# Experts of a two-layer macaron network: routing weights spread by DMA instead of TensorE, gelu left in PSUM, other places for the routing work

## The chip, the cores and the metric

The kernel runs on one core of a Trainium2 chip. The metric is the device time of one execution in microseconds (us); lower is better. PE is TensorE, ACT is ScalarE, DVE is VectorE, POOL is GpSimd, and SP is SyncE, which issues the DMAs.

## The reference

The input `x` has 4096 tokens of 128 channels. Six residual stages follow each other: a gated feed-forward, a time-mixing attention, the feed-forward again, a mixture of experts, a flow attention, and the mixture of experts again. The change is in the fourth and the sixth, which share weights:

```
xn = (x - mu) * rsqrt(var + EPS) * ln_gamma + ln_beta
abel_out = gelu(xn @ abel_w + abel_b)
logits = xn @ moe_gate_w + moe_gate_b
topw, topi = top_k(logits, 2);  topw = softmax(topw)
w_dense = sum(one_hot(topi, 8) * topw[..., None], axis=-2)
h  = gelu(einsum('bsd,edh->ebsh', xn, ew1) + eb1)     # 8 experts, 256 hidden
eo = einsum('ebsh,ehd->ebsd', h, ew2) + eb2
moe_out = einsum('ebsd,bse->bsd', eo, w_dense)        # then three 128x128 rotations
gate = sigmoid(concat(abel_out, moe_out) @ gc_w + gc_b)
x = x + 0.5 * (residual + abel_out * (1 - gate) + moe_out * gate)
```

## The kernel before

Every stage goes through the tokens in 8 chunks of 512 (`NCH`), channels on the partitions. Each engine has its own program, and semaphores tie them together; the order on an engine is written out by hand. The residual `X` stays in SBUF, and SP stores it chunk by chunk in the last stage.

In an expert stage (`experts`, once on each engine) a chunk has 16 units `u` (`NU`): 8 experts of two halves of 128 hidden channels. A unit goes through five steps:

- PE: the first product, three float16 matmuls of 512 columns (`three`, lines L1457 to L1459), into one of banks 0 to 2 (`MM1_BANK`);
- ACT: gelu out of that bank into the buffer `mo.hf` (L980), called gelu(u) below;
- DVE: times the routing weight, `mo.hw` (L1296), called hw(u);
- ACT: the float16 copy `mo.hhi` (`high`, L975), called high(u), in ACT's program behind gelu(u+1);
- POOL: the remainder `mo.hlo` (`low`, L772); then PE's second product (`second`, again three matmuls) into bank 5, `SKEW` units behind the first.

The routing weight of a token must stand on all 128 partitions. PE makes it: for each expert a matmul with the selection matrix `sel` (L1639) copies one row of `mo.wT` over bank 3 or 4. `mo.wT` holds 16 rows in float16 (high and low parts of 8 weights).

`pipeline` runs each step of the loop over three chunks: `lead` (chunk i+1: normalise into `Z`, turn it on PE, take `mo.xn`, `mo.xhi`, `mo.xlo` from bank 6, update `X` by L1315, make the logits and the top-2 chain on DVE, L1328 to L1343, then the weights, L1347 to L1351, and their turned copy `mo.wT`, L1362), `mid` (the 16 units of chunk i), and `lag` (chunk i-1: `mo.dm` L1290, `mo.gs` L1302, the gate on PE and ACT, `mo.r` L1320 and L1323, the addition to `X` L1187, in the fourth stage with the norm's statistics behind it, L1150). At which unit each of these stands is a number in the program (`u == 8`). Of the 8 chunks, six pass through a full step; the first has no lag, the last no lead. At the last unit PE waits until `X` is updated (bank 6 must be free), then makes the Abel product, whose gelu (L998) and scaled copy (L1001) ACT does before high(15).

## Time and profile before

| | us |
|---|---|
| median of 3 runs | 1070.07 (1068.48 to 1070.43) |
| profiled execution, its own time | 1070.72 |
| its span | 1069.0 |
| busy in the span: PE, DVE, ACT, POOL | 878.7, 727.8, 657.3, 604.1 |
| fourth stage, hw(0) of the first chunk to the last pair of hw | 335.0 to 565.6 |
| sixth stage, hw(0) of the first chunk to hw(15) of the last | 829.9 to 1055.7 |

The execution's own time is 1.7 us above its span. No engine is busy all the time: an expert stage is a chain that goes round between engines, and what matters is which engine's program is without a gap at which place of a chunk.

### The profile page before, as it was taken

The numbers are of one execution on the slowest core, as the hardware profiler recorded it, in microseconds if no ns is written. First come the engines' busy times: TensorE is split into PE (matmuls) and PEld (weight loads), VectorE is DVE, ScalarE is ACT, GpSimd is POOL, SyncE is SP. The second block draws the span as 40 slices with busy tenths as digits, with TensorE's granted clock in tenths as the row PEclk, the third lists the DMA queues.
The fourth block names the chain that finished last, engine by engine and source line by source line (L and its number), as shares of the span: only waits on it lengthen the run. The fifth ranks groups of instructions, "written<-read, shape, count | busy, mean of one in ns | idle before, by whom it ended". The sixth has DMA issues, their size and how long they took to land.

```text
span 1069.0 us, 14730 instructions
## 1 busy us (share of the span) xinstructions
PE 878.7 (82%) x3958; PEld 463.0 (43%) x3958; DVE 727.8 (68%) x1580; ACT 657.3 (61%) x1171; POOL 604.1 (57%) x579
## 2 busy tenths in 40 slices
PE   7789677689936988899895698999973899999997
PEld 6644333274412344444442355555532344444443
DVE  6945389945634677887764267777783777777784
ACT  2177499857725777777773443333322778787874
POOL 4244775665484656666676154444446566666664
PEclk9989888769977999999997899999996899999998
DMA  8000000000000000000000000000000000000000
GB/s 201 10 2 0 0 0 1 0 1 2 0 0 1 1 1 1 0 0 0 0 1 1 0 1 0 1 1 1 2 1 0 1 1 11 10 10 10 10 10 20
DMA packets 17932, 8.26 MB, mean 8 GB/s; under 512 B 4168, under 2 KB 17884, under 8 KB 17884
## 3 DMA queue, kind: packets, MB, share of 16 engines
q1 hardware_dynamic: 17884, 7.70, 2.8%
q8 instruction: 21, 0.34, 0.1%
q14 instruction: 27, 0.22, 0.1%
HBM read 5.60 MB, written 2.10 MB: 7 GB/s over the span
## 4 chain that ended last, share of the span: by engine, by line
POOL 33%; issue 29%; PE 18%; DVE 12%; ACT 5%; POOLq 1%; SPq 1%; DVEq 0%; DMA 0%; ACTq 0%
POOL arena L772 19%; POOL arena L792 5%; POOL arena L735 4%; PE bank L1457 3%; PE bank L1458 3%; PE bank L1459 3%; PE bank L1692 3%; POOL rstd L692 2%; POOL v L700 1%; DVE stats L1150 1%; DVE X L1315 1%; ACT arena L975 1%; ACT Z L891 1%; DVE arena L1242 1%; DVE arena L1296 1%
## 5 line engine op out<-in xcount | busy, mean ns | idle before, releaser
L772 POOL TENSOR_TENSOR arena<-arena 128x512 f16<-128x512 f32 x256 | 300.4, 1184 | 181.8 <-ACT arena L975 181.1
L1296 DVE TENSOR_TENSOR arena<-arena,bank 128x512 f32<-128x512 f32 x256 | 172.3, 683 | 93.3 <-ACT arena L980 89.7
L975 ACT ACTIVATE arena<-arena 128x512 f16<-128x512 f32 x256 | 160.4, 627 | 65.4 <-DVE arena L1296 45.2
L980 ACT ACTIVATE arena<-bank,eb 128x512 f32<-128x512 f32 x256 | 173.8, 680 | 34.9 <-PE bank L1459 32.7
L799 POOL TENSOR_TENSOR arena<-arena 128x512 f32<-128x512 f32 (+1 forms) x24 | 32.7, 1374 | 117.7 <-DVE arena L1421 90.0
L1458 PE MATMUL bank<-arena,ew1hi 128*128 128x512 f16 x256 | 99.0, 387 | 0.0
L1457 PE MATMUL bank<-arena,ew1hi 128*128 128x512 f16 x256 | 99.0, 387 | 0.0
L1459 PE MATMUL bank<-arena,ew1lo 128*128 128x512 f16 x256 | 98.9, 386 | 0.0
L1457 PE MATMUL bank<-arena,ew2hi 128*128 128x512 f16 x256 | 97.6, 381 | 0.8 <-POOL arena L772 0.8
L1458 PE MATMUL bank<-arena,ew2hi 128*128 128x512 f16 x256 | 97.5, 381 | 0.0
L1459 PE MATMUL bank<-arena,ew2lo 128*128 128x512 f16 x256 | 97.5, 381 | 0.0
L735 POOL TENSOR_TENSOR arena<-arena 128x512 f16<-128x512 f32 x48 | 54.9, 1159 | 64.4 <-ACT arena L905 64.4
L1639 PE MATMUL bank<-arena,sel 128*128 128x512 f16 x128 | 49.8, 389 | 33.1 <-DVE arena L1296 23.6
L1699 PE MATMUL bank<-arena,until 128*128 128x512 f32 x128 | 63.0, 615 | 14.2 <-DVE arena L1377 13.1
L1457 PE MATMUL bank<-arena,f0hi 128*128 128x512 f16 x144 | 56.9, 395 | 17.0 <-POOL arena L735 13.6
L792 POOL TENSOR_TENSOR arena<-arena 128x1024 f32<-128x1024 f32 x32 | 61.7, 1950 | 0.0
L1211 DVE SCALAR_TENSOR_TENSOR arena<-bank,arena 128x512 f32<-128x512 f32 x48 | 33.0, 691 | 36.0 <-ACT arena L912 34.7
L1388 DVE SCALAR_TENSOR_TENSOR arena<-arena,bank 128x1024 f32<-128x1024 f32 x16 | 19.5, 1221 | 55.3 <-PE bank L1692 55.3
L891 ACT ACTIVATE Z<-X,nbias,rstd 128x128 f32<-128x128 f32 (+1 forms) x128 | 52.5, 487 | 7.4 <-POOL pool_spare L705 7.4
L1541 PE MATMUL bank<-ident,Z 128*128 128x128 f32 x192 | 31.5, 290 | 30.6 <-ACT Z L891 18.1
L1458 PE MATMUL bank<-arena,f0hi 128*128 128x512 f16 x144 | 56.6, 393 | 0.0
L1459 PE MATMUL bank<-arena,f0lo 128*128 128x512 f16 x144 | 56.5, 392 | 0.0
(286 smaller groups left out, 1922.2 us busy)
## 6 DMA issues: line engine op xcount, KB each, us to landing
X<-in_L_attn_x_dram SPq DMA_DIRECT2D x8, 256.0 KB, 4.4
out_dram<-X SPq DMA_DIRECT2D x8, 256.0 KB, 2.3
arena<-in_L_ffn_ew_dram SPq DMA_DIRECT2D x2, 512.0 KB, 6.7
arena<-in_L_ffn_ew_dram SPq DMA_DIRECT2D x1, 1024.0 KB
arena<-in_L_ffn_gens_dram SPq DMA_DIRECT2D x1, 192.0 KB, 2.3
arena<-in_L_ffn_w_gate_dram SPq DMA_DIRECT2D x1, 192.0 KB, 2.7
arena<-in_L_ffn_w_up_dram SPq DMA_DIRECT2D x1, 192.0 KB, 2.8
arena<-in_L_ffn_w_down_dram SPq DMA_DIRECT2D x1, 192.0 KB, 3.9
```

The source lines that it names most:

```text
L735: pool.tensor_tensor(f0.hlo[:, u, :], f0.h[:, u % 2, :], f0.hhi[:, u, :], ALU.subtract).then_inc(S.hlo, 1)
L772: pool.tensor_tensor(mo.hlo[:, u % 8, :], mo.hw[:, u % 4, :], mo.hhi[:, u % 8, :], ALU.subtract).then_inc(S.hlo, 1)
L792: pool.tensor_tensor(fl.kv[:, b, :].rearrange("p (h m d) -> p h m d", d=HD, m=HD), key.to_broadcast([P, HEADS, HD, HD]), value.to_broadcas ...
L891: last = A(Z[:, zp, t * P:(t + 1) * P], X[:, bass.ds(tile * P, P)], ACT.Identity, bias=bias[:, bass.ds(tile, 1)], scale=scale[:, bass.ds(t ...
L975: A(mo.hhi[:, u % 8, :], mo.hw[:, u % 4, :], ACT.Copy).then_inc(S.hhi, 1)
L980: A(mo.hf[:, u % 4, :], bank[MM1_BANK[u]][:, :], ACT.Gelu, scale=1.0 / WS, bias=eb1[:, u:u + 1]).then_inc(S.gelu, 1)
L1296: TT(mo.hw[:, u % 4, :], mo.hf[:, u % 4, :], bank[3 + (u // EB) % 2][:, :], ALU.mult)\
L1457: mm(dst, whi, xhi, start=start, stop=False, skip_group_check=True)
L1458: mm(dst, whi, xlo, start=False, stop=False, skip_group_check=True)
L1459: return mm(dst, wlo, xhi, start=False, stop=stop, skip_group_check=True)
L1639: mm(bank[3 + e % 2][:, :], sel[:, e, :], mo.wT[:, p, :], start=True, stop=True)\
L1699: mm(bank[5 + h], until[:, :], fl.kv[:, b, h * CH:(h + 1) * CH], start=True, stop=True)\
```

## The change

- The weight rows are now float32, 8 of them. DVE makes twice the weight (two small operations fewer, L1349 and L1351 go); the factor 0.5 moves into `mo.dm`. PE turns it, and DVE copies 8 rows of 512 into `mo.wT`.
- SP (`routes`) writes these rows to a scratch tensor in DRAM, waits for it, and issues four DMAs that each read two experts' rows onto all 128 partitions of the new buffer `mo.wB` (512 KB each). DVE waits for the first at unit 0, the next at units 4, 8 and 12. The eight `sel` matmuls a chunk go, and so do `sel` and `ident16` in the setup.
- Banks 3 and 4 are free, so the first products use five banks. ACT writes gelu back into the bank, and DVE multiplies out of it; a bank is free after hw instead of after gelu. `SKEW` is 6.
- The bias of the second product is one float32 matmul (`ebw`) instead of two float16 ones.
- In `lead`, other units: normalise in units 0 and 1 (two tiles each); PE's turn 5 to 3; `xn`, `xhi`, `xlo` 6 to 4; logits and top-2 chain 8 to 5; tanh 10 to 7; weights 11 to 8; PE's turn of the weights 14 to 10; `mo.wT` 14 to 11; the update of `X` 7 to 12.
- SP's loop over the stores is unrolled, with `routes` of the next chunk ahead of each wait and store.

```diff
-SKEW = 5
-MM1_BANK = (0, 1, 2, 0, 1, 2, 0, 1, 2, 0, 1, 2, 0, 1, 2, 1)
+SKEW = 6
+MM1_BANK = (0, 1, 2, 3, 4, 0, 1, 2, 3, 4, 0, 1, 2, 3, 4, 2)
...
-            with sp.Fori(0, NCH) as c:
+            def routes(c):
+
+                sp.wait_ge(MO.wT, c + 1)
+                for k in range(E // 2):
+                    after(sp, MO.wB[k], 16 * c)
+                sp.dma_start(wrows[c % 2], mo.wT[0:E, c % 2, :]).then_inc(MO.wd, 16)
+                sp.wait_ge(MO.wd, 16 * (c + 1))
+                after(sp, MO.hw, NU * (c - 1))
+                for k in range(E // 2):
+                    sp.dma_start(mo.wB[:, c % 2, 2 * k:2 * k + 2, :],
+                                 wrows[c % 2, 2 * k:2 * k + 2, :].partition_broadcast(P)).then_inc(MO.wB[k], 16)
+
+            for c in range(NCH):
+                routes(c)
+            routes(NCH)
+            for c in range(NCH):
+                if c + 1 < NCH:
+                    routes(NCH + c + 1)
                 sp.wait_ge(MO.x, c + (NCH + 1))
-                sp.dma_start(out_parts[:, :, bass.ds(c, 1), :], X4[:, :, bass.ds(c, 1), :]).then_inc(stored, 16)
+                sp.dma_start(out_parts[:, :, c:c + 1, :], X4[:, :, c:c + 1, :]).then_inc(stored, 16)
...
-                            after(act, S.hw, NU * i + u - 3)
-                            A(mo.hf[:, u % 4, :], bank[MM1_BANK[u]][:, :], ACT.Gelu, scale=1.0 / WS,
+                            A(bank[MM1_BANK[u]][:, :], bank[MM1_BANK[u]][:, :], ACT.Gelu, scale=1.0 / WS,
                               bias=eb1[:, u:u + 1]).then_inc(S.gelu, 1)
                             if u:
                                 high(i, u - 1)
-                        if lead and mid and u < TILES:
-                            normalise(i + 1, 1 - p, S.z, first, number, [u])
-                        if lead and u == 6:
+                        if lead and mid and u < TILES // 2:
+                            normalise(i + 1, 1 - p, S.z, first, number, [2 * u, 2 * u + 1])
+                        if lead and u == 4:
                             act.wait_ge(S.tr, i + 2)
                             A(mo.xn, bank[6][:, :], ACT.Copy).then_inc(S.xn, 1)
                             A(mo.xhi[:, 1 - p, :], bank[6][:, :], ACT.Copy).then_inc(S.xhi, 1)
...
+                            if u % (2 * EB) == 0:
+                                dve.wait_ge(S.wB[u // (2 * EB)], 16 * i + 16)
                             after(dve, S.hlo, NU * i + u - 3)
-                            TT(mo.hw[:, u % 4, :], mo.hf[:, u % 4, :], bank[3 + (u // EB) % 2][:, :], ALU.mult)\
+                            TT(mo.hw[:, u % 4, :], bank[MM1_BANK[u]][:, :], mo.wB[:, p, u // EB, :], ALU.mult)\
                                 .then_inc(S.hw, 1)
 
                         if lag and u == 4:
...
                             dve.wait_ge(S.g0, i)
                             STT(out=mo.gs, in0=mo.dm, scalar=gcw[:, 1:2], in1=mo.g0[:, n, :], op0=ALU.mult,
                                 op1=ALU.add).then_inc(S.gs, 1)
-                        if lead and u == 6:
+                        if lead and u == 4:
...
-                        if lead and u == 7:
+                        if lead and u == 12:
...
-                        if lead and u == 8:
+                        if lead and u == 5:
                             own.at(i + 1)
...
-                        if lead and u == 11:
+                        if lead and u == 8:
                             dve.wait_ge(S.th, i + 2)
                             share = mo.th.rearrange("p (t o) -> p t o", o=1).to_broadcast([P, TILES, E])
                             own.link(TT(mo.wd, mo.diff, share, ALU.mult))
-                            own.link(TT(mo.wd, mo.wd, mo.sum, ALU.add))
-                            own.link(TS(mo.wp[:, :, 0:E], mo.wd, 0.5, None, ALU.mult))
                             own.close()
-                            STT(out=mo.wp[:, :, E:2 * E], in0=mo.wd, scalar=0.5, in1=mo.wp[:, :, 0:E], op0=ALU.mult,
-                                op1=ALU.subtract).then_inc(S.wpair, 1)
+                            TT(mo.wd, mo.wd, mo.sum, ALU.add).then_inc(S.wpair, 1)
...
-                        if lead and u == 14:
+                        if lead and u == 11:
                             dve.wait_ge(S.wpT, i + 2)
-                            dve.tensor_copy(mo.wT[0:2 * E, n, :], bank[7][0:2 * E, 0:CH // 2].bitcast(F16))\
-                               .then_inc(S.wT, 1)
+                            after(dve, S.wd, 16 * i)
+                            dve.tensor_copy(mo.wT[0:E, n, :], bank[7][0:E, :]).then_inc(S.wT, 1)
...
-                TAIL = {0: (11,), 1: (12,), 2: (13, 14), 3: (15,)}
+                TAIL = {0: (10,), 1: (11, 12), 2: (13, 14), 3: (15,)}
 
                 def step(i, p, lead, mid, lag):
                     n = 1 - p
                         pe.wait_ge(S.hlo, NU * c + u + 1)
                         if u == 0:
                             after(pe, S.dm, c)
-                            mm(bank[5][:, :], ebhi[:, :], mo.wT[:, cp, :], start=True, stop=False,
-                               skip_group_check=True)
-                            mm(bank[5][:, :], eblo[:, :], mo.wT[:, cp, :], start=False, stop=False,
+                            mm(bank[5][:, :], ebw[:, :], mo.wT[:, cp, :], start=True, stop=False,
                                skip_group_check=True)
                         three(bank[5][:, :], ew2hi[:, u, :], ew2lo[:, u, :], mo.hhi[:, u % 8, :],
                               mo.hlo[:, u % 8, :], start=False, stop=(u == NU - 1)).then_inc(S.mm2, 1)
                         if mid:
                             if u == 0:
                                 pe.wait_ge(S.xlo, i + 1)
-                            if u % EB == 0:
-                                e = u // EB
-                                if e == 0:
-                                    pe.wait_ge(S.wT, i + 1)
-                                after(pe, S.hw, NU * i + EB * (e - 1))
-                                mm(bank[3 + e % 2][:, :], sel[:, e, :], mo.wT[:, p, :], start=True, stop=True)\
-                                    .then_inc(S.wb, 1)
-                            after(pe, S.gelu, NU * i + bank_free(u))
+                            after(pe, S.hw, NU * i + bank_free(u))
                             three(bank[MM1_BANK[u]][:, :], ew1hi[:, u, :], ew1lo[:, u, :], mo.xhi[:, p, :],
                                   mo.xlo[:, p, :]).then_inc(S.mm1, 1)
                         for v in TAIL.get(u, ()) if lag else ():
                             second(i - 1, n, v)
                         if mid and u >= SKEW:
                             second(i, p, u - SKEW)
-                        if lead and u == 5:
+                        if lead and u == 3:
...
-                        if lead and u == 8:
+                        if lead and u == 5:
                             pe.wait_ge(S.xn, i + 2)
```

On DVE, in the full step of the loop, this is what stood between `mo.xlo` (L1306) and the start of the top-2 chain (L1328) before; L1296 is hw:

```order
L1306 TENSOR_TENSOR arena<-bank,arena 128x512
L1293 REGISTER_ALU
L1296 TENSOR_TENSOR arena<-arena,bank 128x512
L1315 ISA x2
L1315 TENSOR_SCALAR X<-X,keep,shift 128x128
...
L1315 TENSOR_SCALAR X<-X,keep,shift 128x128
L1293 REGISTER_ALU
L1294 REGISTER_ALU
L1296 TENSOR_TENSOR arena<-arena,bank 128x512
L1328 TENSOR_TENSOR arena<-bank,gate_b4 128x32
```

Now, from `mo.gs` (L1298) over `mo.xlo` (L1302) to the chain (L1324 to L1339); hw is L1292:

```order
L1298 SCALAR_TENSOR_TENSOR arena<-arena,gcw 128x512
L1301 REGISTER_ALU
L1302 TENSOR_TENSOR arena<-bank,arena 128x512
L1288 REGISTER_ALU
L1292 TENSOR_TENSOR arena<-bank,arena 128x512
L1324 TENSOR_TENSOR arena<-bank,gate_b4 128x32
...
L1339 TENSOR_TENSOR arena<-arena 128x32
L71 REGISTER_ALU
L1288 REGISTER_ALU
L1292 TENSOR_TENSOR arena<-bank,arena 128x512
```

The chain stands behind hw(5), directly after `mo.gs` and `mo.xlo`, and the update of `X` has left this place. It is now here, between hw(12) and hw(13), behind the copy of the weight rows (L1356) and ahead of the addition to `X` (L1182):

```order
L1356 COPY arena<-bank 8x512
L1288 REGISTER_ALU
L1292 TENSOR_TENSOR arena<-bank,arena 128x512
L1311 ISA
L1311 REGISTER_ALU
L1311 TENSOR_SCALAR X<-X,keep,shift 128x128
...
L1288 REGISTER_ALU
L1292 TENSOR_TENSOR arena<-bank,arena 128x512
L1182 ISA
L1182 SCALAR_TENSOR_TENSOR X<-bank,X 128x512
```

So the last four units of a chunk have the two longest pieces of DVE's other work between them.

On SP, the end of the program before is a loop of 8 stores:

```order
L598 UNCONDITIONAL_BRANCH
L598 ISA
L600 ISA
L600 DMA out_dram<-X 128x4x128
L598 REGISTER_ALU
L598 COMPARE_AND_BRANCH
```

Now, in the sixth stage (`wrows` is the scratch tensor, and the four DMAs of L601 go into `mo.wB`):

```order
L611 DMA out_dram<-X 128x4x128
L597 DMA wrows<-arena 8x512
L601 DMA arena<-wrows 128x1024 x4
L611 DMA out_dram<-X 128x4x128
L597 DMA wrows<-arena 8x512
L601 DMA arena<-wrows 128x1024 x4
```

A write of weight rows has moved behind a store, and the store waits for the addition to `X` of the chunk before. In the fourth stage nothing is stored, and only L597 and L601 follow each other.

## Rows read from the trace of the kernel before

**Rows 1.** The chain of waits: start us, us, what.

```profile
440.63 2.55 issue
...
470.77 2.55 issue
...
933.73 2.55 issue
...
962.96 2.55 issue
```

**Rows 2.** Stretches, fourth stage and end of the sixth; busy (instructions), PE clock.

```profile
core 0: us, PE busy (x) PEld busy (x) DVE busy (x) ACT busy (x) POOL busy (x), PEclk, DMA share, GB/s
454.30:484.50 30.20, 27.10 (x133) 12.77 (x131) 23.72 (x57) 23.16 (x43) 18.94 (x17) 1.00 0.00 0
1034.00:1055.70 21.70, 21.70 (x102) 10.12 (x101) 14.06 (x21) 17.89 (x31) 16.74 (x15) 1.00 0.02 6
```

**Rows 3.** Timeline of DVE, one chunk: start us, us, line, op, [idle before].

```profile
454.34 0.69 DVE L1296 TENSOR_TENSOR arena<-arena,bank 128x512 f32<-128x512 f32 x1 [2.40 <-ACT arena L980]
...
460.48 1.51 DVE L1302 SCALAR_TENSOR_TENSOR arena<-arena,gcw 128x512 f32<-128x512 f32 x1
...
465.46 2.81 DVE L1315 TENSOR_SCALAR X<-X,keep,shift  x4
...
468.79 0.18 DVE L1328 TENSOR_TENSOR arena<-bank,gate_b 128x32 f32<-128x32 f32 x1
...
471.93 1.28 DVE L1296 TENSOR_TENSOR arena<-arena,bank 128x512 f32<-128x512 f32 x2 [0.22 <-DVE arena L1343]
473.13 0.69 DVE L1320 SCALAR_TENSOR_TENSOR bank<-bank,arena 128x512 f32<-128x512 f32 x1
...
475.06 0.69 DVE L1347 TENSOR_TENSOR arena<-arena 128x32 f32<-128x32 f32 x1
475.79 0.19 DVE L1348 TENSOR_TENSOR arena<-arena 128x32 f32<-128x32 f32 x1
...
478.58 0.68 DVE L1187 SCALAR_TENSOR_TENSOR X<-bank,X 128x512 f32 x1
...
480.48 0.69 DVE L1296 TENSOR_TENSOR arena<-arena,bank 128x512 f32<-128x512 f32 x1
```

**Rows 4.** Timeline of ACT, the start of that chunk.

```profile
451.06 0.63 ACT L975 ACTIVATE arena<-arena 128x512 f16<-128x512 f32 x1 [0.81 <-DVE arena L1296]
...
452.93 0.61 ACT L975 ACTIVATE arena<-arena 128x512 f16<-128x512 f32 x1
453.45 0.67 ACT L980 ACTIVATE arena<-bank,eb 128x512 f32<-128x512 f32 x1
454.02 0.48 ACT L891 ACTIVATE Z<-X,nbias,rr 128x128 f32 x1
454.41 0.67 ACT L980 ACTIVATE arena<-bank,eb 128x512 f32<-128x512 f32 x1
```

**Rows 5.** Timeline of PE, that chunk.

```profile
451.60 0.39 PE L1639 MATMUL bank<-arena,sel 128*128 128x512 f16 x1 [1.31 <-DVE arena L1362]
451.82 0.38 PE L1457 MATMUL bank<-arena,ew1hi 128*128 128x512 f16 x1
...
465.21 1.02 PE L1656 MATMUL bank<-arena,ones 128*128 128x512 f32 x2
```

**Rows 6.** DMA issues, KB each, median us from issue to landing.

```profile
out_dram<-X SPq DMA_DIRECT2D x8, 256.0 KB, 2.3
arena<-in_L_ffn_ew_dram SPq DMA_DIRECT2D x2, 512.0 KB, 6.7
...
tvec<-n_L_attn_time_mix_r_dram SPq DMA_DIRECT2D x1, 0.5 KB, 2.1
```

**Rows 7.** Timeline of SP, issue of one DMA.

```profile
7.25 0.43 SPq L567 DMA_DIRECT2D tvec<-n_L_attn_time_mix_r_dram  x1
```

**Rows 8.** Timeline of DVE, before the fourth stage, POOL idle.

```profile
326.11 1.11 DVE L1315 TENSOR_SCALAR X<-X,keep,shift 128x128 f32<-128x128 f32 x4
```

More of the change, by code:

```diff
@@ L181, in macaron_kernel @@
         ablo = sb("ablo", [P, P], F16)
-        ebhi = sb("ebhi", [P, P], F16)
-        eblo = sb("eblo", [P, P], F16)
-        sel = sb("sel", [P, E, P], F16)
+        ebw = sb("ebw", [P, P])
         gamma = sb("gamma", [P, 1])
@@ L260, in macaron_kernel @@
         sm.eb2 = a.take([P], parts=E)
-        sm.eb2T = a.take([2, E])
+        sm.eb2T = a.take([E])
         sm.G = a.take([NROT, P])
@@ L278, in macaron_kernel @@
         mo.xlo = a.take([2, CH], F16)
-        mo.hf = a.take([4, CH])
+        mo.wB = a.take([2, E, CH])
         mo.hw = a.take([4, CH])
@@ L297, in macaron_kernel @@
         mo.wd = a.take([TILES, E])
-        mo.wp = a.take([TILES, 2 * E], F16)
-        mo.wT = a.take([2, CH], F16)
+        mo.wT = a.take([2, CH])
         a = Arena(arena)
@@ L358, in macaron_kernel @@
         S0.rots = sem("setup_rots")
-        S0.turned = sem("setup_turned")
         S0.gtp = sem("setup_gtp")
@@ L437, in macaron_kernel @@
         MO.gelu = sem("moe_gelu")
-        MO.wb = sem("moe_wb")
+        MO.wd = sem("moe_wd")
+        MO.wB = [sem(f"moe_wB{k}") for k in range(E // 2)]
         MO.hw = sem("moe_hw")
@@ L633, in setup @@
                           allow_small_or_imprecise_dtypes=True).then_inc(S0.consts, 1)
-                pool.wait_ge(S0.pool, 7)
-                pool.affine_select(out=sel[:, :, :], in_=sel[:, :, :], compare_op=ALU.not_equal, fill=1.0, base=0,
-                                   pattern=[[-1, E], [0, P]], channel_multiplier=1).then_inc(S0.pool, 1)
+                pool.wait_ge(S0.pool, 5)
                 pool.affine_select(out=blockones[:, :], in_=blockones[:, :], compare_op=ALU.is_ge, fill=0.0,
@@ L657, in bias_parts @@
                 chain = Chain(pool, S0.bias)
-                chain.base = 9
+                chain.base = 6
                 pool.wait_ge(S0.w_flow, 16 * N_FLOW)
@@ L846, in setup @@
                 for r in range(NROT):
-                    act.wait_ge(S0.rtp, r + 1)
-                    A(sm.rr[:, r, P:2 * P], bank[5 + r][:, P:2 * P], ACT.Copy).then_inc(S0.turned, 1)
+                    act.wait_ge(S0.gtp, r + 2)
+                    A(sm.rr[:, r, P:2 * P], bank[5 + r][:, P:2 * P], ACT.Copy).then_inc(S0.gt, 1)
                 act.wait_ge(FF.tr, 1)
@@ L858, in fold_a @@
                 act.wait_ge(S0.small, 1)
-                for n in range(2):
-                    A(sm.eb2T[:, n, :], bank[FOLD.m][:, 0:E], ACT.Copy).then_inc(S0.eb2T, 1)
+                A(sm.eb2T, bank[FOLD.m][:, 0:E], ACT.Copy).then_inc(S0.eb2T, 1)
                 for g in range(NU // TILES):
@@ L867, in fold_a @@
                     if g == 1:
-                        act.wait_ge(S0.rp, 1)
-                        A(sm.R, bank[FOLD.m][:, 0:P], ACT.Copy).then_inc(S0.r, 1)
+                        act.wait_ge(S0.mtp, 2)
+                        A(sm.R, bank[FOLD.m][:, 0:P], ACT.Copy).then_inc(S0.mt, 1)
             def fold_b():
@@ L879, in fold_b @@
                 act.wait_ge(S0.consts, N_CONST)
-                A(ebhi[0:2 * E, :], bank[FOLD.small][0:2 * E, P:2 * P], ACT.Copy, scale=WS)
-                A(sm.MT[0:2 * E, :], bank[FOLD.small][0:2 * E, P:2 * P], ACT.Copy, scale=WS).then_inc(S0.fhi, 1)
+                A(ebw[0:E, :], bank[FOLD.small][0:E, P:2 * P], ACT.Copy, scale=WS).then_inc(S0.fhi, 1)
             def normalise(c, zp, sem, first, number, tiles=range(TILES)):
@@ L992, in step @@
                             A(bank[6][:, :], bank[6][:, :], ACT.Tanh, scale=0.5, bias=gcbh[:, :]).then_inc(S.tg, 1)
-                        if lead and u == 10:
+                        if lead and u == 7:
                             act.wait_ge(S.dtop, i + 2)
@@ L1278, in experts @@
             def experts(S, first, number):
-                own = Chain(dve, S.own, 11)
+                own = Chain(dve, S.own, 9)
                 dve.wait_ge(S.zero, 1 if first == 0 else 2)
@@ L1513, in fold_a @@
                         pe.wait_ge(S0.mt, 1)
-                        mm(bank[FOLD.m][:, 0:P], sm.MT, rot(2), start=True, stop=True).then_inc(S0.rp, 1)
+                        mm(bank[FOLD.m][:, 0:P], sm.MT, rot(2), start=True, stop=True).then_inc(S0.mtp, 1)
                 pe.wait_ge(S0.folds, 2)
@@ L1533, in fold_b @@
                     last.then_inc(S0.fm, 1)
-                mm(bank[FOLD.small][0:2 * E, P:2 * P], sm.eb2T.rearrange("p a b -> p (a b)"), sm.R, start=True,
-                   stop=True).then_inc(S0.fm, 1)
+                mm(bank[FOLD.small][0:E, P:2 * P], sm.eb2T, sm.R, start=True, stop=True).then_inc(S0.fm, 1)
             def turn_chunk(z, zp, sem_z, value, sem_out, to=0):
@@ L1668, in step @@
                             last.then_inc(S.rT, 1)
-                        if lead and u == 14:
+                        if lead and u == 10:
                             pe.wait_ge(S.wpair, i + 2)
-                            turned = bank[7][0:2 * E, 0:CH // 2].bitcast(F16)
                             for t in range(TILES):
-                                last = tr(turned[:, t * P:(t + 1) * P], mo.wp[:, t, :], ident16[:, :])
+                                last = tr(bank[7][0:E, t * P:(t + 1) * P], mo.wd[:, t, :], ident[:, :])
                             last.then_inc(S.wpT, 1)
```

51 lines of the change are left out of this document (18 added, 33 removed).

## Prediction

> **What bounds the kernel now.** I read the chain of waits first. In the expert stages it names POOL and "issue" again and again, at one distance: 470.77 - 440.63 = 30.14 us in the fourth stage, 962.96 - 933.73 = 29.23 us in the sixth [rows 1]. That is a full chunk, and POOL stands there only as the last link. In the view of stretches PE is busy 27.1 of 30.2 us at the full clock, DVE 23.7, ACT 23.2, POOL 18.9 [rows 2], so nobody is the bound alone, and I went to the timelines to see where each engine has no gap. DVE has none from about 464 to 482: update of `X`, top-2 chain, `mo.r`, weights, addition to `X` with statistics, copy of `mo.wT` [rows 3]. Then PE, which has waited 1.31 for that copy, starts the next chunk with `sel` [rows 5], DVE idles 2.40 before hw(0) [rows 3], and PE, nearly without a gap, leads to the turned chunk, `mo.xlo` and DVE again. The round is DVE 17, PE and ACT 13. Only in the last chunk of a stage, which has no lead, is PE busy throughout, 21.70 of 21.70 [rows 2].
>
> **PE's part.** 8 `sel` matmuls and 2 bias ones go, each one step of 451.82 - 451.60 = 0.22 [rows 5]: 2.2 a chunk. One float32 matmul of 512 columns comes, two passes, 1.02 [rows 5], 0.9 of it its own, and 0.1 for the wider turn. Net -1.2 a chunk. It shortens a full chunk only if PE is in the round, and the wait for `mo.wT`, which put it there, is gone. So I go round the new program with the old durations.
>
> **The new round, fourth stage.** ACT first. From high(14) at 451.06 over the Abel gelu, its copy and high(15) at 452.93 to gelu(0) at 453.45 are 2.39 [rows 4], unchanged. Then up to gelu(4): four gelus of 0.57, three copies of 0.52, and the four tiles of the normalise, 0.39 each (454.41 - 454.02) [rows 4], now all in units 0 and 1: 5.4. PE needs 33 matmuls of 0.22 and one turn for gelu(4), some 7.9 from the chunk's start on PE; high(14) comes 1.3 after that start (PE's wait for `X` at the last unit is over before DVE's statistics, 1.9, are), so ACT is at gelu(4) after 1.3 + 2.4 + 5.4 = 9.1 and sets it. gelu to hw takes 0.89 (454.34 - 453.45) [rows 3, 4], and hw(14) to high(14) 0.7 (480.48 against 451.06 + 30.14). ACT's stretch is 9.4.
>
> From hw(4) to hw(14) DVE has hardly a gap: 10 hw of 0.60 (473.13 - 471.93 for two), 6.0; `mo.gs` 1.6 (1.51 in its row); `mo.xlo` 0.6; the top-2 chain 471.93 - 468.79 = 3.1, I take 3.2; the weights, two operations, 0.73 and 0.2 [rows 3], with some blocking 1.1; `mo.r` 475.06 - 473.13 less one hw, 1.3; the copy of 8 float32 rows 0.6, like other 512-column reads from PSUM; `X` 468.79 - 465.46 less one hw, 2.7; addition and statistics 480.48 - 478.58 = 1.9 [rows 3]. Two new gaps come in. During the chain ACT stands in high(6), and gelu(8) is behind it, so after hw(6) and hw(7) DVE waits 1.1 for gelu(8); before hw(10), ACT's tanh of the gate costs 0.6. In the old order `mo.r` and the weights filled such holes. Sum 20.7, and a chunk 9.4 + 20.7 = 30.1: no gain against 30.14, though DVE is rid of 1.4 and PE of 1.2. I give this walk 0.5 a chunk both ways.
>
> The spread is hidden there. `mo.wT` is ready near hw(12); write and first broadcast take some 6, and 9.5 are left before hw(0) is wanted. Four broadcasts of 512 KB fit in 30 us even at the loaded rate of 6.7 each [rows 6].
>
> **Sixth stage.** No statistics: 1.3 less. But there SP goes store by store: weights of the next chunk are ready before the addition to `X`, yet their write stands behind a store that waits for this addition. From the end of the addition: waking SP 0.1, issue of the store 0.43 [rows 7], write of the rows 2.1 (the row of 0.5 KB) and 0.3 for the 256 KB of the store ahead of it [rows 6], waking SP and DVE 0.2, and the broadcast L: 3.1 + L. L is bounded by 2.3 (256 KB on an idle queue) and 6.7 (512 KB on a full one) [rows 6]; the queue is idle here, so I take 3.2, a fifth of the way from the idle row to the loaded one (512 KB are twice the idle row's bytes). The round is then hw(0) to hw(4) 5.2 (0.8 to high(0), 3.5 of ACT, 0.9), hw(4) to hw(13) 20.7 - 0.6 - 1.9 = 18.2, hw(13) and addition 1.3, spread 6.3: 31.0 against 29.23, +1.8. With L 2.3 it is 30.1, +0.9; with 6.7 34.5, +5.3. What is queued behind hw(0) on DVE is everything; ACT stops in high(0) after gelu(1), and PE after five first products.
>
> The Trainium skill has a price for this ("DMA: Bandwidth & Descriptors", section "Anatomy of one DMA"): about 2.0 us fixed and the bytes over 436 GB/s, for GpSimd's queue, most of it the confirmation of the write, longest for HBM. An estimate by that page is 2.0 for the write and 3.2 for the broadcast, which gives this sum, 1073; by the 6.7 of [rows 6] it would be 1094. The row of 0.5 KB, 2.1, agrees with the page's fixed part.
>
> **Ends and setup.** First chunk: the chain comes before the update of `X`, which alone takes 1.1 [rows 8], and two small operations fewer; PE waits no longer for weights, but hw(0) waits for the spread: -0.7 each, from -2.5 to +2.5. Last chunk: PE's, so its 1.3 of matmuls (1.2 without the turn) and the 1.3 wait [rows 5] go, -2.6; in the sixth stage PE also gives back 0.9 of the late hw(0), -3.5. In the setup POOL's `sel` goes where POOL waits anyway; fewer copies in the weight folding, -0.3.
>
> **Sum.** Fourth stage -0.7 + 0 - 2.6 = -3.3; sixth -0.7 + 6 x 1.8 - 3.5 = +6.6; setup -0.3: +3.0 on the execution's 1070.7, which stands 0.65 above the median: 1073.
>
> **A rule that speaks for more.** Beside POOL the four tiles of `X` take 2.81 [rows 3], alone 1.11 [rows 8], so 1.7 of DVE's 20.7 is blocking, about 0.9 for each of two POOL operations, and it hangs on where these fall. The skill ("SBUF — State Buffer", section "Who interferes with whom") says that such operations and POOL's exclude each other for a whole instruction. By it each of the chain's cast, `mo.gs`, the two weight operations and `X` could be hit in the new places; three more hits are 2.6 a chunk and 30 in all, one is 0.9 and 11. No row shows where POOL's operations will fall, so this is in the range, not in the sum.
>
> **Rivals.**
> - *The stretches overlap (faster).* If the five banks let PE and ACT run so far ahead that DVE's gaps fill and hw(4) isn't held by ACT, a chunk falls to what PE allows: 27.1 - 1.2 and about 1.3 of waiting for the update of `X` at the last unit, with 0.8 of other stalls 28.0. Then 6 x 2.1 + 6 x 1.2 + 8 at the ends is -28: 1042; half of it, 1056. For it: PE's busy share and 2.6 less work on two engines. Against it: ACT does gelu and high strictly in turn. It decides from the point where ACT's and DVE's stretches together are under 28.
> - *The spread is hidden in the sixth stage too.* With L near 2.3 and the walk 0.3 too long, gains at the ends and losses cancel: 1070.
> - *The broadcast is slow.* All 128 partitions read the same 4 KB; if that takes the loaded 6.7, it is +21 more: 1094. One more blocking by POOL a chunk, +11, ends at 1084.
> - *The change doesn't do what it says:* PE cannot run ahead because its second products still wait for POOL; that is the walk's result already.
>
> **How the numbers follow.** My forecast, 1073 (its own range 1067 to 1081), 0.50; overlap 0.22; hidden 0.16; slow broadcast or more blocking 0.12. The range goes from 1056 to 1088. 0.2% (2.1 us) is about what a measurement tells from no change. Faster: 0.22, some of "hidden" and a little of the forecast, 0.28. Same: 0.17. Slower: 0.55.
>
> **What would show it.** Right: chunks of 30 us in the fourth and 31 in the sixth stage; DVE waiting for a DMA before hw(0) in the sixth only, by 1 to 3 us; DVE gaps before hw(8) and hw(10); PE idle before the logits and before the Abel product; the last chunk about 3 shorter. Wrong: a chunk under 29 in the fourth (the walk), or no wait for the DMA in the sixth (L or the order on SP), or waits at units 4, 8 and 12 (bandwidth).

## The result, and the profile after

The changed kernel takes 1080.26 us, median of 4 runs (1079.92 to 1083.16), against 1069.28 (1068.21 to 1070.43) for the kernel before on the same chip: ratio 1.0092, 95% interval 1.0058 to 1.0126. It is slower, inside the range, and 7 us above the forecast of 1073.

The spans of the two profiled executions, 1069.0 and 1078.7, were compared stretch by stretch, by the starts of the first hw (`hw(0)`) of each chunk; a last chunk is counted to the end of its hw(15):

| stretch | before | after | difference | forecast |
|---|---|---|---|---|
| up to 300 us, no expert work | | | +2.8 | -0.3 |
| fourth stage, to hw(0) of its second chunk | | | +0.2 | -0.7 |
| its six middle chunks | 6 x 30.10 | 6 x 30.37 | +1.6 | 0 |
| its last chunk | 22.44 | 19.87 | -2.6 | -2.6 |
| fifth stage, and sixth to hw(0) of its second chunk | | | +2.5 | -0.7 |
| six middle chunks of the sixth | 6 x 29.19 | 6 x 30.52 | +8.0 | +10.8 |
| its last chunk | 22.36 | 19.60 | -2.8 | -3.5 |

They add to 9.7, the difference of the spans.

The view of stretches of the changed kernel, for a middle chunk of the fourth and of the sixth stage (us of the stretch, busy time of each engine, granted clock), answers to [rows 2]:

```profile
457.44:487.74 30.30, 27.42 (x124) 12.78 (x123) 23.24 (x54) 23.20 (x44) 18.62 (x16) 0.94 0.19 69
951.75:982.33 30.58, 25.86 (x125) 12.39 (x123) 21.92 (x49) 23.17 (x44) 18.53 (x16) 1.00 0.24 78
```

PE, the first figure, has only 25.86 us to do in the sixth stage, 1.2 less than in [rows 2] as forecast. In the fourth it shows 27.42 for the same work, and the granted clock, 0.94, is not full. That was not forecast. DVE's timeline of the same chunk of the fourth stage, in the places of [rows 3]:

```profile
458.29 0.69 DVE L1292 TENSOR_TENSOR arena<-bank,arena 128x512 f32<-128x512 f32 x1 [2.67 <-ACT bank L975]
...
463.49 0.69 DVE L1292 TENSOR_TENSOR arena<-bank,arena 128x512 f32<-128x512 f32 x1 [0.21 <-ACT bank L975]
464.10 1.74 DVE L1298 SCALAR_TENSOR_TENSOR arena<-arena,gcw 128x512 f32<-128x512 f32 x1
...
470.14 1.42 DVE L1292 TENSOR_TENSOR arena<-bank,arena 128x512 f32<-128x512 f32 x2 [0.19 <-DVE arena L1339]
472.25 0.69 DVE L1292 TENSOR_TENSOR arena<-bank,arena 128x512 f32<-128x512 f32 x1 [0.69 <-ACT bank L975]
...
474.07 0.19 DVE L1345 TENSOR_TENSOR arena<-arena 128x32 f32<-128x32 f32 x1
...
475.98 0.69 DVE L1292 TENSOR_TENSOR arena<-bank,arena 128x512 f32<-128x512 f32 x1 [0.98 <-ACT bank L975]
...
479.71 2.56 DVE L1311 TENSOR_SCALAR X<-X,keep,shift  x4
```

The two gaps that the walk named are there, before hw(8) and hw(10). But behind the second stands PE. Its timeline shows a wait for the input of the logits, and then every matmul at twice its time: the bias product takes 1.91 and the next steps 0.43 in place of 0.22 [rows 5]. The row below them is the view of stretches of that time, and its granted clock is a half (1.2 GHz):

```profile
464.56 1.06 PE L1643 MATMUL bank<-gate_g,arena 128*128 128x8 f32 x8 [1.82 <-ACT arena L983]
...
466.18 1.91 PE L1615 MATMUL bank<-arena,ebw 128*128 128x512 f32 x2
467.89 0.63 PE L1450 MATMUL bank<-arena,ew2hi 128*128 128x512 f16 x1
468.32 0.63 PE L1451 MATMUL bank<-arena,ew2hi 128*128 128x512 f16 x1
```

```profile
466.10:469.40 3.30, 3.30 (x7) 1.10 (x6) 3.12 (x20) 1.29 (x2) 2.31 (x2) 0.50 0.00 0
```

All six middle chunks of the fourth stage and its first have such a stretch, and none of the sixth's middle ones. But the same wait is in those too, for 1.82 us as well, and what follows it there runs at the full clock:

```profile
961.58 1.06 PE L1643 MATMUL bank<-gate_g,arena 128*128 128x8 f32 x8 [1.82 <-ACT arena L983]
962.50 0.38 PE L1450 MATMUL bank<-arena,ew1hi 128*128 128x512 f16 x1
...
963.14 1.02 PE L1615 MATMUL bank<-arena,ebw 128*128 128x512 f32 x2
```

So the wait alone does not decide it. What else does, no run here isolates.

In the sixth stage the chain of waits shows the spread, link by link, from the addition to `X` to hw(0):

```profile
978.63 0.69 DVE X L1182
979.32 0.02 issue
979.34 0.39 SPq L611
...
979.89 1.89 DMA wrows<-arena
981.79 0.02 issue
981.80 4.29 DMA arena<-wrows
...
986.21 0.70 DVE arena L1292
```

And the view of waits puts 37.1 us on it, in seven waits, six in the sixth stage and one in the fourth stage's first chunk:

```profile
DVE arena L1292 <- DMA arena<-wrows: 37.1, 7, 5.6
```

### The profile page after: what moved, and what is told of

The parts are those of the page before. It is cut to its first block, busy times and chain, and to the rows that moved or that the text cites. A ratio compares the mean times of both kernels' runs of the same rounds, so it can differ in the third digit from the quotient of the medians.

```text
span 1078.7 us, 14118 instructions
## 1 busy us (share of the span) xinstructions
PE 871.6 (81%) x3821; PEld 462.6 (43%) x3830; DVE 720.1 (67%) x1548; ACT 656.9 (61%) x1169; POOL 596.3 (55%) x572
## 4 chain that ended last, share of the span: by engine, by line
issue 28%; POOL 24%; DVE 18%; PE 17%; ACT 8%; DMA 3%; SPq 1%; DVEq 1%; POOLq 0%; ACTq 0%
POOL arena L770 10%; POOL arena L790 4%; POOL arena L733 4%; DVE arena L1292 3%; PE bank L1674 3%; PE bank L1450 2%; DMA arena<-wrows 2%; PE bank L1452 2%; PE bank L1451 2%; ACT bank L975 2%; POOL rstd L694 2%; ACT arena L971 2%; ACT Z L887 1%; POOL v L702 1%; DVE stats L1145 1%
## 5 line engine op out<-in xcount | busy, mean ns | idle before, releaser
L1292 DVE TENSOR_TENSOR arena<-bank,arena 128x512 f32<-128x512 f32 x256 | 171.9, 684 | 121.6 <-ACT bank L975 76.8
L975 ACT ACTIVATE bank<-bank,eb 128x512 f32<-128x512 f32 x256 | 167.0, 653 | 41.0 <-PE bank L1452 36.1
L1370 DVE TENSOR_TENSOR arena<-bank,arena 128x512 f32<-128x512 f32 x64 | 42.4, 686 | 12.9 <-PE bank L1681 12.9
```

Source lines behind the costliest of these rows:

```text
L975: A(bank[MM1_BANK[u]][:, :], bank[MM1_BANK[u]][:, :], ACT.Gelu, scale=1.0 / WS, bias=eb1[:, u:u + 1]).then_inc(S.gelu, 1)
L1292: TT(mo.hw[:, u % 4, :], bank[MM1_BANK[u]][:, :], mo.wB[:, p, u // EB, :], ALU.mult)\
L1370: TT(fl.prod[:, b % 2, h * CH:(h + 1) * CH].rearrange("p (h m d) -> p h m d", d=HD, m=HD), bank[5 + h].rearrange("p (h m d) -> p h m d", d ...
```

## The experiments

Ratios are to the kernel before, which ran beside each; "chunk" is a middle one, from the profile. `after` stands for the changed kernel.

**SP's order (`sp_ahead`).** In the sixth stage:

```diff
+            routes(NCH + 1)
             for c in range(NCH):
-                if c + 1 < NCH:
-                    routes(NCH + c + 1)
+                if c + 2 < NCH:
+                    routes(NCH + c + 2)
```

> In the sixth stage SP issues the weights' write and broadcasts of the next chunk but one ahead of the store that waits for the addition to X, everything else as changed. Theory (SP's order costs the sixth stage): DVE's wait of 5.5 us for the DMA before hw(0) goes; ACT's own start of a chunk then ends the wait after about 2.7 us as in the fourth stage, and DVE's stretch is that of the fourth less 1.3 of statistics: chunk 29.1 against 30.6 us, 6 x 1.5 = 9 us, and 1 at the last chunk: about 1071. Rival (the DMA's wait only hides what ACT or PE would make DVE wait anyway, and the unit order of DVE sets 30.6): chunk stays within 0.3, 1079 to 1080.

Measured: 1067.24, ratio 0.9979 (0.9964 to 0.9994). No DVE wait for the DMA is left in the middle chunks; hw(0) waits 2.53 for ACT. The theory's wait is gone, and the time is 4 us below what it said: the chunks are 29.06, 27.89, 28.12, 29.35, 28.00 and 29.17, two kinds, where one of 29.1 was expected. The view of stretches for one of each:

```profile
888.32:916.21 27.89, 25.41 (x124) 12.37 (x122) 21.95 (x49) 23.17 (x43) 18.55 (x16) 1.00 0.24 76
944.33:973.68 29.35, 27.54 (x126) 12.87 (x124) 22.26 (x49) 23.32 (x43) 18.64 (x16) 0.94 0.29 89
```

The long ones are those with part of the time at the half clock. In this run's fourth stage five middle chunks of six have it and take 30.1 to 30.7; the one without takes 29.2. So the half clock seemed to cost some 1.2 us a chunk, and the next runs asked whether that is cause or sign.

**Three banks (`banks3`).** `MM1_BANK` as before the change.

> The changed kernel with the first products in three banks (as before) in place of five, skew and everything else as changed. Theory (PE running ahead is worth nothing, since ACT stands in high(0) and DVE has the long stretch): chunks 30.4 and 30.6 as with five, 1080 within 2 us. Rival (the five banks do carry part of the round, since PE's run ahead hides its wait for the turned chunk and the logits): 0.5 to 1 us more for each of the 12 middle chunks, 1086 to 1092.

Measured: 1088.57 (1079.48 to 1091.18), ratio 1.0158 (1.0104 to 1.0213). The rival, in one stage: the fourth is about as with five banks (29.1 to 30.4), the sixth has 30.7 to 33.5, and its granted clock is where the time is:

```profile
919.50:953.20 33.70, 30.10 (x127) 13.80 (x126) 22.49 (x49) 23.92 (x45) 18.59 (x16) 0.90 0.22 71
```

This looks like the rival. But the changed kernel, run again (below), had three such chunks with five banks too, and its interval overlaps this one. That five banks hold the clock through the wait before hw(0) more often than three is left open; that they are worth more than a few us here is not shown.

**DVE's stretch (`fill`).** The update of `X` goes from unit 12 to unit 1, and in the fourth stage:

```diff
-                            if first == 0:
-                                finish_x(i - 1, first, bank[6][:, :], 0.5, S.x, i)
-                            else:
-                                add_to_x(i - 1, first, bank[6][:, :], 0.5, S.x, number)
+                            add_to_x(i - 1, first, bank[6][:, :], 0.5, S.x, 0 if first == 0 else number)
+                        if lag and u == NU - 1 and first == 0:
+                            wait_apart(dve, S.x, i)
+                            tile_stats(i - 1 - first)
```

> The changed kernel with two pieces of DVE's long stretch moved to where DVE idles: the update of X from unit 12 to unit 1, and in the fourth stage the statistics from unit 13 behind hw(15), where DVE waits 2.7 us for the next chunk. Theory (the round is DVE's stretch from hw(4) to hw(14) and ACT's from there): X leaves 2.6 in the fourth and 1.7 in the sixth stage, of which about 1 comes back as later hw(2) and hw(3), the statistics leave 1.1: the fourth stage's chunk falls from 30.4 to about 28.2, the sixth's from 30.6 to about 29.9, together 17 us: 1063. Rival (PE, with the logits' wait of 1.8 and the turn behind the later ACT, becomes the bound): fourth stage 29.5, sixth 30.6, 1075.

Measured: 1066.03, ratio 0.9966 (0.9945 to 0.9986); fourth stage 28.0 to 28.6, about as the theory had it. `X` is also cheaper in unit 1, away from POOL's operations: 1.11 in place of 2.56. The sixth stage, where the theory had 29.9, stays at 30.1 to 30.7, with one of 32.8: DVE finished earlier, but hw(0) still waits for the DMA, and now the half clock has come in there too (0.94 in a middle chunk).

**Logits later on PE (`logits_late`).** The block of the logits goes from the end of unit 5 to unit 6, behind its first product.

> The changed kernel with PE's logits one unit later, behind the first product of unit 6, so that PE waits less for ACT's copy (1.8 us in front of the logits, after which the granted clock fell to a half for some microseconds in every middle chunk of the fourth stage). Theory (the walk's 30.1 against the 30.4 measured is this lower clock): granted clock full, chunk 30.1, sixth stage unchanged, about 1078. Rival (PE is outside the round, the clock costs nothing, the 0.3 is elsewhere): chunk 30.4, 1080; or, if the chain on DVE starts later for it, 0.3 a chunk more, 1084.

Measured: 1071.57, ratio 1.0012 (0.9999 to 1.0026). Fourth stage 28.9 to 29.5 in the three middle chunks at the full clock, 29.7 to 29.9 in the three that still have a stretch at the half. The mechanism held and its size did not. The profiled execution is 12.2 us shorter than that of the changed kernel: 5.3 are the middle chunks of the fourth stage, where the theory had 2 by taking 0.3 for what the clock costs, and 4.8 lie ahead of the stage, where the two kernels are the same.

**More work for PE (`warm`).** Cause or sign, in one edit:

```diff
+                        if lead and mid and u == 5:
+                            for w in range(6):
+                                mm(bank[7][:, :], ew1hi[:, w, :], mo.xhi[:, p, :], start=True, stop=True)
                         if lead and u == 5:
                             pe.wait_ge(S.xn, i + 2)
```

> The changed kernel with six extra matmuls of 512 columns (1.3 us at the full clock, written to a bank that the logits overwrite) on PE in front of its wait for the logits' input, where it idles 1.8 us. Order, places, DMA and SP as changed. Theory (this idle time takes PE's clock to a half for 3.4 us in each middle chunk of the fourth stage, and the half clock itself costs the chunk 1.2 us: the run with SP's order had one chunk without it, of 29.2 against 30.4): the clock stays full, the fourth stage's chunk falls to 29.2 though PE has more to do, the sixth's stays at 30.6, about 1072. Rival (the late logits cost, not the clock): chunk 30.4 or, by the extra 1.3 on PE, up to 30.9: 1080 to 1084.

Measured: 1068.85 (1066.78 to 1072.89), ratio 0.9998 (0.9984 to 1.0012). PE does six matmuls more in each such chunk, which nobody needs, and the kernel takes 10 us less than without (by the ratios, 0.9998 and 1.0092). 6.8 of them are the fourth stage's middle chunks. The rest isn't shown to be the edit's: the profiled executions also differ by 2.5 ahead of the stage and by 4.3 between hw(15) of the fourth stage and the first copy of `mo.wT` in the sixth, where the code is the same, and that second stretch takes anything from 256.3 to 261.3 us in the thirteen profiles with the changed setup. The middle chunks of the fourth stage are 28.9 to 29.3 (the first 29.6), the sixth's 30.2 to 30.9. PE's rows in the place of those above, and the stretch of one chunk:

```profile
456.95 1.46 PE L1642 MATMUL bank<-arena,ew1hi 128*128 128x512 f16 x6
458.94 1.06 PE L1646 MATMUL bank<-gate_g,arena 128*128 128x8 f32 x8 [0.53 <-ACT arena L983]
...
460.50 1.02 PE L1615 MATMUL bank<-arena,ebw 128*128 128x512 f32 x2
```

```profile
451.81:481.09 29.28, 27.42 (x131) 12.90 (x130) 22.82 (x54) 23.03 (x44) 18.42 (x16) 1.00 0.24 83
```

The logits start 1.06 us after hw(4) here and 1.07 in the changed kernel (464.56 - 463.49). So the input comes no later than before, and the late input costs nothing; what follows at the half clock does. In both stages of this run no middle chunk has a stretch at the half clock. The theory holds.

**First broadcast halved (`first_small`).** Experts 0 and 1 in broadcasts of their own.

> The changed kernel with the weights of experts 0 and 1 in broadcasts of their own (256 KB each), the others in pairs as before. Theory (hw(0) in the sixth stage and in each stage's first chunk waits for issue, write and the first broadcast in a row, and of its 4.3 us about half goes with the bytes): the wait before hw(0) falls from 5.5 to about 4.0, the sixth stage's chunk from 30.6 to about 29.3 if nothing else is late, 8 chunks x 1.3 = 10 less, 1070. Rival (the 4.3 us are mostly fixed, or the four queued broadcasts share the DMA engines from the start): at most 0.5 a chunk, 1076 to 1080; or expert 1 is late at hw(2) and gives it back.

Measured: 1076.10, ratio 1.0055 (1.0034 to 1.0076). The wait before hw(0) falls from 5.5 to 4.6 in the sixth stage, so a broadcast of 256 KB needs about 0.9 us less than one of 512 KB, and by that difference more than half of 4.3 us is not bytes (an estimate; no run issues one broadcast alone, so what the ones queued behind it take is in it). In the middle chunks nothing of it arrives: they are 30.1 to 31.2, and five of six now have a stretch at the half clock:

```profile
948.28:979.15 30.87, 27.54 (x125) 13.00 (x123) 22.41 (x49) 23.20 (x43) 18.59 (x16) 0.94 0.23 77
```

**Old places (`places_before`).** The routing and the update of `X` in the units of before, all else changed.

> The changed kernel (DMA for the weights, gelu in PSUM, five banks) with the routing and the update of X in the units where they stood before: turn 5, logits and chain 8, weights 11, turn and copy of the weights 14. Theory (the spread takes about 6.5 us from the copy to hw(0), and from unit 14 there are only 3.4, so the DMA's wait comes into every chunk of both stages; what was moved is what hides it in the fourth): both stages wait for the DMA before hw(0), chunk about 31.5 to 32.5 in the fourth and about 31 in the sixth, about 1090. Rival (the old places suit the round, the new gaps before hw(8) and hw(10) cost as much as the spread): 30.4 in the fourth, 1078 to 1082.

Measured: 1094.85, ratio 1.0232 (1.0215 to 1.0249). Chunks 31.8 to 32.5 and 30.5 to 32.2; the wait for the DMA is now in 15 places, both stages:

```profile
DVE arena L1292 <- DMA arena<-wrows: 73.2, 15, 5.9
```

The theory holds. The new places hide the spread in the fourth stage, as the prediction said, and save some 11 to 15 us, by the two measurements of the changed kernel.

**Gelu in SBUF (`gelu_sbuf`).** Four buffers as before; PE's bank comes free after the gelu.

```diff
-                            A(bank[MM1_BANK[u]][:, :], bank[MM1_BANK[u]][:, :], ACT.Gelu, scale=1.0 / WS,
+                            after(act, S.hw, NU * i + u - 3)
+                            A(mo.hf[:, u % 4, :], bank[MM1_BANK[u]][:, :], ACT.Gelu, scale=1.0 / WS,
...
-                            TT(mo.hw[:, u % 4, :], bank[MM1_BANK[u]][:, :], mo.wB[:, p, u // EB, :], ALU.mult)\
+                            TT(mo.hw[:, u % 4, :], mo.hf[:, u % 4, :], mo.wB[:, p, u // EB, :], ALU.mult)\
...
-                            after(pe, S.hw, NU * i + bank_free(u))
+                            after(pe, S.gelu, NU * i + bank_free(u))
```

> The changed kernel with the gelu's output in SBUF again (four buffers), so that PE's next use of a bank waits for the gelu and no longer for hw; DMA, five banks and places as changed. Theory (PE's waits for banks are outside the round; a gelu to SBUF takes 0.68 in place of 0.65, some 0.1 for the four in ACT's stretch, 0.5 for the chunk): chunks 30.4 to 30.6 and 30.6 to 30.8, 1080 to 1082. Rival (banks that come free one operation earlier keep PE fed while hw(0) is late, or fill its waits and save the clock in the fourth stage): 29.3 in the fourth stage, 1072.

Measured: 1126.00, ratio 1.0520 (1.0505 to 1.0535). Both expectations missed by over 40 us. hw now reads two operands from SBUF (`arena<-arena`), where it had one in PSUM (`arena<-bank,arena`). The groups of hw and of POOL's `low` in this kernel, then in the changed one:

```profile
L1294 DVE TENSOR_TENSOR arena<-arena 128x512 f32<-128x512 f32 x256 | 228.7, 912 | 113.7 <-ACT arena L977 77.3 <-DMA arena<-wrows 30.2 <-issue 4.3
L771 POOL TENSOR_TENSOR arena<-arena 128x512 f16<-128x512 f32 x256 | 334.1, 1319 | 205.3 <-ACT arena L972 203.2
```

```profile
L1292 DVE TENSOR_TENSOR arena<-bank,arena 128x512 f32<-128x512 f32 x256 | 171.9, 684 | 121.6 <-ACT bank L975 76.8
L770 POOL TENSOR_TENSOR arena<-arena 128x512 f16<-128x512 f32 x256 | 297.2, 1170 | 190.4 <-ACT arena L971 186.8
```

hw takes 0.91 us on the mean (0.67 to 1.68) in place of 0.68, `low` 1.32 in place of 1.17. The Trainium skill ("SBUF — State Buffer", section "Who interferes with whom") has this rule: a VectorE operation with two inputs in SBUF contends with a GpSimd operation that reads SBUF, one with at most one, outside the modes that take both of VectorE's ports, does not. The trace agrees: with one input in PSUM none of the 256 hw takes over 0.70. Of the 46 us between the profiled executions 33 are in the middle chunks and 13 in the two last ones. The half clock is in most of them too (all but one of the middle chunks and both last ones), and no run separates the two; the one middle chunk without it takes 33.5, against 31.0 in the same place of the changed kernel. Once the weights lie in SBUF, the gelu in PSUM is what keeps the change from costing 5%. That a gelu to PSUM is itself shorter, 0.653 against 0.679, is small beside it.

**The change again (`after_again`).** No edit. (The folding is the small matmuls of the setup, near 220 us, that combine weights. Of the eight variants run before it, five had it at the higher clock and three had not.)

> The changed kernel once more, unedited. Asked: the first profile of it showed 2.9 us lost in the weight folding near 220 us, where the granted clock stayed at a half for 23.9 us in place of 10.2, and five of the seven variants with the same setup do not show it. Theory (an event of single executions, not of the change): the new profile has 10.2 or 23.9 by chance, its chunks are 30.4 and 30.6 as before, the median of all its runs is 1077 to 1081. Rival (it belongs to the change, and the variants shifted it away): 23.9 again and 1080 to 1081 in nearly every run.

Measured: 1083.55 (1075.78 to 1085.94), ratio 1.0115 (1.0090 to 1.0141). The median is above what either expectation had, and the folding's clock is low again, as the rival had it; see below. The fourth stage repeats (30.3 to 30.7, one of 29.2, one of 31.8). The one of 29.2 is the same program, with the same wait of 1.82 before the logits, and the full clock:

```profile
485.47:514.68 29.21, 25.75 (x124) 12.30 (x123) 23.02 (x54) 23.07 (x43) 18.50 (x17) 1.00 0.21 70
```

The sixth has 30.7, 30.1, 30.7 and then 33.6, 33.7 and 31.6, with this in one of them:

```profile
957.50:966.00 8.50, 8.08 (x24) 4.03 (x25) 6.71 (x26) 3.98 (x8) 3.46 (x4) 0.60 0.00 0
```

So the spread of 10 us between runs of the changed kernel, where the kernel before has 3, is at least in part the half clock in more or fewer chunks. The mean granted clock of each run goes with it: 0.918 in the run of 1075.78 and 0.904 to 0.909 in the other five, 1082.23 to 1085.94.

**Both repairs (`two_repairs`).** `sp_ahead` and `warm` together, nothing moved.

> The changed kernel with only its two faults repaired, nothing moved: SP's order one chunk ahead in the sixth stage, and the six extra matmuls in front of the logits' wait in both expert stages. Theory (what the change loses is the DMA's wait of the sixth stage and the half clock, and nothing else): every middle chunk of the fourth stage 29.2, of the sixth 27.9, granted clock 1.00 in both, so 6 x 1.1 + 6 x 2.7 = 23 us under the changed kernel, 1056 to 1060. Rival (the extra 1.3 us of PE's work, or another wait, takes part of it back in the sixth stage once the chunk is so short): 28.6 to 29.2 there, 1061 to 1066.

Measured: 1055.88 (1053.21 to 1058.08), ratio 0.9877 (0.9860 to 0.9894). Fourth stage 28.9 to 29.5, sixth 27.9 to 28.1; two stretches of about a chunk, one in each stage:

```profile
424.00:453.00 29.00, 27.03 (x130) 12.91 (x129) 22.80 (x55) 22.86 (x43) 18.53 (x16) 1.00 0.18 73
924.00:952.00 28.00, 26.65 (x131) 12.94 (x129) 21.88 (x50) 23.09 (x43) 18.46 (x17) 1.00 0.23 85
```

The theory, at its lower edge. What the change loses in its middle chunks is these two things: with both repaired a chunk takes 29.2 and 28.0 on the mean, 0.9 and 1.1 less than in the kernel before.

**Together (`combo`)** are `sp_ahead`, `fill` and `logits_late`.

> The three edits that helped alone, together: SP's order one chunk ahead, update of X in unit 1 and statistics behind hw(15), logits one unit later. Theory (they act on different waits, and PE's clock stays nearly full with fewer waits): fourth stage's chunk 28.0, sixth 27.2, about 1040. Rival (PE, busy 25.9 at the full clock, loses the clock in each chunk to waits that the shorter DVE stretch does not fill): 28.5 in both, about 1052.

Measured: 1050.84, ratio 0.9817 (0.9787 to 0.9847). Chunk 27.9 in both stages, at the full clock but for one; the rival's time for another reason. DVE was no longer the long stretch: PE waited 0.81 for the logits' input and 1.38 for the weights to turn.

**One turn later (`combo2`).** On top of it, PE's turn of the weights goes from unit 10 to 11 and DVE's copy from 11 to 12.

> The three edits together (chunk 27.9 in both stages, PE busy 25.7 of it at the full clock) and the turn of the weights on PE one unit later, with DVE's copy: PE waits 1.4 us for it in front of the turn. Theory (PE is now in the round, with waits of 0.8 for the logits' input and 1.4 for the weights): 1.0 to 1.4 a middle chunk, 12 of them, 12 to 17 us, 1034 to 1039. Rival (ACT with high and gelu in strict turn and DVE's chain still set the round, PE only waits in it): chunk 27.7 to 27.9, 1049 to 1051.

Measured: 1037.77 (1036.99 to 1041.93), ratio 0.9698 (0.9684 to 0.9712), the fastest version. The wait for the turn is gone, PE's other two, 0.81 and 0.63, remain:

```profile
416.56:444.02 27.46, 25.93 (x125) 12.39 (x123) 21.64 (x54) 22.97 (x43) 18.99 (x17) 1.00 0.23 79
924.09:951.55 27.46, 25.94 (x125) 12.38 (x123) 20.86 (x50) 22.98 (x43) 18.99 (x17) 1.00 0.26 85
```

The chunk fell only 0.4, 5 us in all; the other 8 lie outside the middle chunks, and part of them lies ahead of the expert work (in the profiled executions the fourth stage's first hw(0) comes 3.9 us earlier), so this run confirms the sign and not the size of its theory, though its time lies inside the theory's range.

## Why the prediction was right, and where it was not

**Fourth stage, the walk.** Forecast 30.1, measured 30.37. In the chunk from 458.29 ACT's stretch, hw(14) to hw(4), measured 9.2 (forecast 9.4), DVE's 21.15 (20.7). But the sum came out near by luck. At the full clock, in `warm` and in one chunk of `after_again`, DVE's stretch is 20.1 and the chunk 29.2; the walk is 0.9 long, 5.5 us over six chunks. The half clock then adds 1.1 a chunk, nearly 7 us, and the two errors cancel. Without the second the kernel would have been level with the one before (`warm`, 0.9998), and 1073 would have been some 4 us too slow.

Where the 1.1 arises is not one place. The gelus behind the stretch at the half clock wait for PE, and DVE waits 0.98 for ACT before hw(10); but hw(10) comes 12.5 us after hw(4) where it comes at 12.2 in the full-clock chunk of `after_again`, only 0.3 apart (in two of `warm`'s six chunks it comes at 11.5, and there it is all of it). The other 0.9 is the update of `X`. In the full-clock chunk of `after_again` one of POOL's operations runs beside the second weight operation, and `X` meets one fewer:

```profile
501.25 1.07 DVE L1345 TENSOR_TENSOR arena<-arena 128x32 f32<-128x32 f32 x1
...
506.56 1.69 DVE L1311 TENSOR_SCALAR X<-X,keep,shift  x4
```

With the half clock these two take 0.19 and 2.56 (474.07 and 479.71 above). So the clock costs time also by moving DVE's operations against POOL's, which is the effect that the prediction had put in its range and not in its sum. The step that failed: PE's share was priced at the full clock of [rows 2], and what PE's new waits do to that clock stood in the sum at nothing.

**Fourth stage, the spread hidden.** Right: only the first chunk waits for the DMA, and `places_before` shows the other case.

**Sixth stage, SP's order.** Right, and the largest term. Forecast 31.0, measured 30.5 on the mean. The parts were not each right: in the chunk from 955.54 hw(0) to hw(4) 5.0 (5.2), hw(4) to hw(13) 17.5 (18.2), hw(13) and addition 1.2 (1.3), spread 7.0 (6.3), 30.7 in all. DVE's part is shorter than forecast and the spread longer, so that the sum came out 0.5 near is in part luck. In the spread the write took 1.9 where 2.4 was put, the first broadcast 4.3 where L was 3.2, so L is the term that was mis-sized, inside its bounds of 2.3 and 6.7; it came out nearly half of the way from the idle row to the loaded one, where a fifth was taken. The estimate by the Trainium skill's page "DMA: Bandwidth & Descriptors" (section "Anatomy of one DMA") had 3.2 as well and was 1.1 low. `sp_ahead` gives 2 us a chunk back. Of the 5.5 us that DVE idles before hw(0), 2.5 stay there as a wait for ACT, so the DMA adds 3, the upper end of the sign that the prediction named. No wait for a DMA stands at units 4, 8 or 12.

**Ends.** The last chunks -2.6 and -2.8 for -2.6 and -3.5: PE's terms were right; the late hw(0) was not given back. The first chunks were forecast 0.7 shorter each. In both, copy to hw(0) takes 6.5, against 3.8 before; the fourth stage's came out 0.2 longer, and the sixth stage's, with the fifth before it, 2.5, of which 0.8 lies before the copy of `mo.wT`, within what that stretch varies between executions. Together they are 4.1 over the forecast: the wait for the spread, which was in the bound of +2.5 each and not in the sum.

**What was not in it.** 2.9 us were lost near 220 us, in the weight folding. Both kernels run the same small matmuls there; the view of stretches, of before and of after:

```profile
219.00:225.00 6.00, 6.00 (x41) 5.81 (x41) 3.03 (x3) 4.42 (x5) 4.58 (x4) 0.78 0.01 3
```

```profile
219.00:225.00 6.00, 6.00 (x28) 5.61 (x27) 3.33 (x4) 4.70 (x6) 4.29 (x4) 0.50 0.01 3
```

The clock rose later, and 28 matmuls ran where 41 had. Of the thirteen profiles with the changed setup six show this and seven do not. Kernels with the same code up to there differ in it, so that code alone does not bring it; both profiles of the changed kernel itself show it, so whether it goes with the execution or with the program isn't shown. Whether the kernel before ever has it is open too: there is one profile of it, without, and its 3 us of spread leave little room.

**The rivals.** Overlap (1042, 1056): `two_repairs` has its time, 1056, and not its mechanism. In its sixth stage the two stretches still stand end to end, 9.5 and 18.7, 28.1 together, so nothing overlaps that did not before; it's the walk, without the spread and the half clock. The hidden spread in the sixth stage did not happen, and the slow broadcast did not either: the first one took 3.7 to 4.4, and the median of all four 5.5. Blocking by POOL grew little in sum: in the new places `X` shows 2.56 (2.81 in [rows 3]), `mo.gs` 1.74 (1.51), the first weight operation 1.18 (0.69). That the banks do not let PE run ahead to any use was the walk's result; `banks3` did not clearly contradict it.

## What to carry to other kernels

An engine's idle time off the critical path is free only while it doesn't change the engine: for PE ask, for each new wait, what the granted clock shows behind it, and price the work there at both levels. A queue that both feeds the next step and stores the last one should do the feeding first. The trip write, wait, broadcast was some 6 to 7 us here from the last producer, and halving the first broadcast took only 0.9 off it. When an operand moves from PSUM to SBUF, look at where the same instruction's other operand lies, and at what POOL does beside it.

## What was unexpected of the hardware

Six needless matmuls of 512 columns, 1.46 us of PE, took 7 us off the fourth stage's middle chunks, since no stretch at half the clock followed the wait any more. The same wait of 1.82 us was followed by the half clock in some chunks of one kernel and not in others. A 512 KB broadcast of 4 KB of DRAM, the first of four issued together, took 3.7 to 4.4 us, of which half the bytes save only 0.9. hw with two operands in SBUF beside POOL took up to 1.68 us against 0.68, and POOL's operation lost 0.15 as well.
